# Last pair of the first deformable convolution: 24 halves and 13 gathered tiles in place of 16 and 17

## The chip, the cores and the metric

The kernel runs on one core of one Trainium2 chip. The metric is the time of one execution in microseconds (us), measured on the device. A core has five engines that work side by side, each through its own instructions in order, tied by semaphores: TensorE (PE in the rows, its weight loads PEld), VectorE (DVE), ScalarE (ACT), GpSimd (POOL) and SyncE (SP), which here only issues DMAs.

## The reference, cut to what matters

Two blocks work on 8 images of 32 channels and 80 x 80 pixels. The second has two deformable convolutions, here called C1 and C2; each samples, for each pixel and each of nine taps, the input at a place that a small convolution has computed, weighs it with a mask, and sums over taps and channels:

```python
def modulated_deform_conv(x, offset, mask, weight):
    ...
    py = ys - PAD + ki + off[:, :, 0]      # row of each tap's sample
    px = xs - PAD + kj + off[:, :, 1]      # column
    samp = bilinear_gather(x, py, px)      # four corners, weighted
    samp = samp * mask[:, None]
    return jnp.einsum('bckhw,ock->bohw', samp, weight.reshape(Co, Cx, KK))

om1 = conv2d(x, w_om1, b_om1)
out = modulated_deform_conv(x, offset1, mask1, w_dcn1)     # C1
out = jax.nn.gelu(batchnorm(out, ...))
out = modulated_deform_conv(out, offset2, mask2, w_dcn2)   # C2
x = x + jax.nn.gelu(batchnorm(out, ...) + identity)
```

## The kernel before

The images are worked on as four pairs (p = 0 to 3). In C1 a pair's pixels are sampled in one of two ways.

A **gathered tile** has 16 x 16 pixels of both images. GpSimd fetches the four corners of each sample from a table in memory with 36 indirect DMAs (L900), nine for each of four units, into one set of buffers G; a unit's buffer is free again when VectorE has summed the unit. VectorE computes the places (`locate`, `index`, `weigh`) two tiles ahead, multiplies the corners by their weights (L2139, `scale`) and adds them in pairs (L2153, `part`); TensorE turns and adds the parts (L1157, `turn_unit`), ScalarE copies the sample (L1542), TensorE projects it (L1244, `project_tile`).

A **half** has two rows of 64 pixels of both images and no gather. Offsets reach a few rows and columns only, so TensorE multiplies, for each tap, column weights TX1 (loaded by DMA and shaped by ScalarE, L1489 and L1491) with the columns of the table XT1 (`taps_half`, L1216; BTP are its two PSUM banks, one for each side). VectorE multiplies the 15 rows that come out by row weights TY1 (`weight_half`, L2250) into a product buffer for each side, and TensorE sums over the rows in transposing matmuls (`reduce_half`, L1229, 15 of them for each side and group of three taps). ScalarE copies the sample (L1712), TensorE projects it (`project_half`, L1253). Offsets, mask and row weights of two halves are made at a time (`prepare_half_strips`, L1898 to L1916; convolution L1091 and L1097, turning L1040).

Which pixels are halves is in `C1_ROWS`: for each pair a range of rows, columns 0 to 63. Rows 32 to 63 of the last pair make 16 halves; the other 17 tiles are gathered.

The order is written by hand: `schedule` calls, for every engine, the same list of steps, and `mix` reads a string. "g" is a gathered tile alone (`consume`), "f" a gathered tile with a half beside it, their instructions interleaved (`consume_both`), "d" and "x" belong to the first block's dense convolution, which is over before the last pair. The last pair's strings before are "gf", "ff", "ff", then three times "fff", then "ff"; behind each but the last stand three of the nine steps (`build_step`, L968) that build a table for C2. Behind the stage come `unlend`, `calibrate` and `columns`, and then C2's rounds, each with a gathered tile and a strip.

Of the kernel before, what the change touches and what calls it, by code (L numbers as in the profile page):

```python
# [9 lines left out]
PAIRS = 4  # L10
P = IMG * C
R2 = 2 * C
# [37 lines left out]
C1_ROWS = {0: (32, 48), 1: (32, 48), 2: (32, 48), 3: (32, 64)}  # L50
# [22 lines left out]
def build_program(nc, x, w_off, b_off, w_dcn, par, ident_d, base_y_d, base_x_d, bbase_d, out):  # L73
# [10 lines left out]
    with ctx:  # L84
# [60 lines left out]
        def lender(p):  # L145
            return 1 if p == 0 else 0
# [6 lines left out]
        TX1F = {p: [lent(lender(p), lent_at(p) + 128 * k0, 128 * (k1 - k0)) for k0, k1 in TX_TAPS] for p in C1_ROWS}  # L153
        TX1 = {p: lent(lender(p), lent_at(p), 128 * TAPS).rearrange("p (k b n) -> p k b n", k=TAPS, b=2) for p in C1_ROWS}
        TY1 = {p: lent(lender(p), lent_at(p) + 1152, IDXS * WY1).rearrange("p (n w) -> p n w", w=WY1) for p in C1_ROWS}
# [60 lines left out]
        TAP = BTP + [OUT[1]]  # L216

# [139 lines left out]
        def column_groups(p):  # L357
            first, end = C1_ROWS[p]
            r0, r1 = first - 1 - BELOW1, end + 1 + WY1 - 1 - BELOW1
            return r0, [(r, min(8, r1 - r)) for r in range(r0, r1, 8)]  # L360
# [64 lines left out]
        def mix(on, c, kinds, gseg, at, dseg, at_d, cseg, at_c, then=""):  # L425
            before = ()
            for i, kind in enumerate(kinds):
                seg = dseg if kind == "d" else gseg
                done = sum(k != "d" for k in kinds[:i])
                done_d = sum(k in "dx" for k in kinds[:i])  # L430
                t = done_d + at_d if kind == "d" else done + at
                halves = at_c + kinds[:i + 1].count("f")
                ahead = (cseg, halves) if (kinds + then)[i + 1:i + 2] == "f" else None
                closes = i + 1 == len(kinds)
                prep = after_next(seg, t, c.n)
# [66 lines left out]
        def schedule(eng, on):  # L502
# [14 lines left out]
            for p in C1_ROWS:  # L517
# [155 lines left out]
        def _(sp):  # L673
# [93 lines left out]
            class on:  # L767
# [40 lines left out]
                def consume_both(step, half):  # L808
                    if half.prep:
                        on.prepare(*half.prep)  # L810
# [126 lines left out]
        def _(pe):  # L937
            class on:
# [265 lines left out]
                def taps_half(half, k):  # L1204
# [5 lines left out]
                    if h or k:  # L1210
                        pe.wait_ge(weighted1, 18 * h + 2 * k)
                    row = strip_row(seg, t // 2) + t % 2 * 2 + k // 3 - 1 - BELOW1 - r0
                    for side in range(2):
                        ps_ = slice(XW * side, XW * side + XW)
                        for im in range(2):
                            last = nc.tensor.matmul(BTP[side][64 * im:64 * im + 64, 0:TAPW1], TX1[p][ps_, k, im, :],  # L1216
# [31 lines left out]
                def project_half(half):  # L1248
                    pe.wait_ge(main.samp_ready, half.v + 8)
# [8 lines left out]
                def consume_both(step, half):  # L1258
# [35 lines left out]
                    on.project_half(half)  # L1294

# [141 lines left out]
        def _(act):  # L1437
            class on:
# [262 lines left out]

                def consume_both(step, half):
# [4 lines left out]
                    def half_sample(gr):  # L1707
                        act.wait_ge(prod_used, step.wg + 2 * (gr + 1) + GROUPS)
                        if gr == 0:
                            act.wait_ge(main.projected, step.v + 2)  # L1710
                        from_ = RED[1][0:TPG * C, 0:256].rearrange("p (h n) -> p h n", h=2)
                        last = nc.scalar.activation(SAMP1[half.seg.p][:, gr], from_, ACT.Copy)  # L1712
                        if gr < GROUPS - 1:
                            last.then_inc(group_sampled, 1)
                        else:
                            last.then_inc(main.samp_ready, 2)

# [3 lines left out]
                    half_sample(0)  # L1721
# [3 lines left out]
                    half_sample(1)  # L1725
# [6 lines left out]
                    half_sample(2)  # L1732
# [20 lines left out]
        def _(dve):  # L1753
# [15 lines left out]
            class on:  # L1769
# [104 lines left out]
                def columns1(p, built, halves):  # L1874
# [5 lines left out]
                    r0, groups = column_groups(p)  # L1880
                    for j, (row, count) in list(enumerate(groups))[1::2]:
# [4 lines left out]
                def prepare_half_strips(seg, t, q, n, cs):  # L1886
# [5 lines left out]
                    ty, lent_ = TY1[seg.p], LENT[seg.p]  # L1892
# [14 lines left out]
                    if cs:  # L1907
                        dve.wait_ge(weighted1, 36 * cs)
# [334 lines left out]
                def weight_half(half, k):  # L2243
                    gr, j, p = k // TPG, k % TPG, half.seg.p
                    for side in range(2):
                        at = 2 * gr + side
                        if j == 0:
# [4 lines left out]
                            in0=BTP[side][:, 0:TAPW1].rearrange("p (w c) -> p w c", w=WY1),  # L2252
                            in1=TY1[p][:, (half.t % 2 * 2 + side) * TAPS + k, :].unsqueeze(2).to_broadcast([128, WY1, C]),
                            op=ALU.mult).then_inc(weighted1, 1)

# [186 lines left out]
```

## Time and profile before

| | us |
|---|---|
| median of 3 runs | 6645.84 |
| lowest and highest | 6641.96, 6651.39 |
| the profiled execution | 6641.73 |
| its span | 6639.8 |
| busy: TensorE | 5752.4 (87%) |
| busy: GpSimd | 4601.9 (69%) |
| busy: VectorE | 4548.5 (69%) |
| busy: ScalarE | 2140.5 (32%) |

A busy share is an average over the whole span. What an edit in one stage is worth has to be read in that stage: which engine is never idle, and which wait ends last. The last pair of C1 begins with its first gather at 3448.6 us of the span and ends with its last half's projection at about 4240.8.

### The profile page before, as it was taken

To read this page: it belongs to the slowest core of one execution; us is meant where nothing else is said; L and a number is where in the kernel's file an instruction comes from. 1 tells how busy PE (TensorE), PEld (TensorE's weight loads), DVE (VectorE), ACT (ScalarE), POOL (GpSimd) and SP (SyncE) were. 2 spreads that over 40 slices of the span, in tenths; PEclk is the share of its full clock that TensorE was granted. 3 is DMA by queue.
4 is the path that set the end of the run, shared out by engine and by line. 5 is a ranking of instruction groups with operands and counts; after the bars stand their busy time and mean duration, and the time that the engine had idled before them with its cause. 6 is when DMAs were issued, how large, how long until landed. Compare 5 with 4: busy or idle time off the path is not lost. (4 is left out here: it accounts for less than half of the span.)

```text
span 6639.8 us, 129061 instructions
## 1 busy us (share of the span) xinstructions
PE 5752.4 (87%) x50305; PEld 4624.7 (70%) x50305; DVE 4548.5 (69%) x8684; ACT 2140.5 (32%) x3416; POOL 4601.9 (69%) x4765
## 2 busy tenths in 40 slices
PE   6997888987888988888977777799989989998996
PEld 6886776766777757777754555577767767776775
DVE  6886776866777857777854555577666766776775
ACT  1222222222222222222222222254434444443442
POOL 0005777777777777777777777777777777777776
PEclk9997999998999989999978888899989989998998
DMA  5333343435343433443332222333333333333333
GB/s 149 100 100 108 106 113 110 116 88 143 103 113 107 116 88 105 111 110 102 106 84 78 74 71 74 93 88 88 84 90 94 91 80 103 91 88 86 89 85 76
DMA packets 511330, 647.82 MB, mean 98 GB/s; under 512 B 118856, under 2 KB 414120, under 8 KB 502824
## 3 DMA queue, kind: packets, MB, share of 16 engines
q0 software_dynamic: 152064, 311.73, 18.6%
q1 hardware_dynamic: 358696, 328.04, 17.5%
q8 instruction: 412, 6.75, 0.4%
q14 instruction: 158, 1.29, 0.1%
HBM read 593.26 MB, written 46.15 MB: 96 GB/s over the span
## 5 line engine op out<-in xcount | busy, mean ns | idle before, releaser
L900 POOL DMA_INDIRECT G<-table,IDX x4752 | 4587.8, 965 | 1992.9 <-issue 1930.8
L2340 DVE TENSOR_TENSOR ARENA<-ARENA,OUT 128x864 f32<-128x864 f32 x936 | 937.9, 1048 | 130.6 <-PE RED L1142 97.8
L2139 DVE TENSOR_TENSOR G<-G,WPS 128x1152 f32<-128x1152 f32 x528 | 711.5, 1348 | 432.9 <-DMA G<-table,IDX 431.7
L1547 ACT ACTIVATE SAMP<-RED 96x384 f32<-96x384 f32 x688 | 335.4, 487 | 1907.2 <-PE RED L1365 815.8
L1142 PE MATMUL RED<-IDENT,ARENA 128*96 128x128 f32 x7344 | 880.6, 280 | 76.2 <-DVE ARENA L2340 76.2
L1142 PEld LDWEIGHTS RED<-IDENT,ARENA 128*96 128x96 f32 x7344 | 820.6, 129 | 121.1 <-issue 117.4
L1346 PE MATMUL BTP<-PAD,ARENA 80*128 x2304 | 744.9, 446 | 56.1 <-DVE ARENA L2132 29.5
L1091 PE MATMUL OFF<-PAD,ARENA 128*54 128x128 f32 (+1 forms) x10944 | 740.9, 293 | 19.5 <-ACT PAD L1447 6.8
L1091 PEld LDWEIGHTS OFF<-PAD,ARENA 128*54 128x54 f32 (+1 forms) x10944 | 659.9, 133 | 128.5 <-issue 98.9
L1216 PE MATMUL BTP<-X 64*64 64x480 f32 x2880 | 396.4, 621 | 199.5 <-DVE ARENA L2250 139.6
L1542 ACT ACTIVATE SAMP<-RED 96x384 f32<-96x384 f32 x448 | 218.3, 487 | 1068.6 <-PE RED L1157 547.9
L1346 PEld LDWEIGHTS BTP<-PAD,ARENA 80*128 80x128 f32 x2304 | 398.0, 193 | 185.7 <-issue 95.1
L1355 PE MATMUL RED<-IDENT,ARENA 128*96 128x128 f32 x3840 | 497.3, 277 | 0.0
L1355 PEld LDWEIGHTS RED<-IDENT,ARENA 128*96 128x96 f32 x3840 | 423.5, 127 | 83.1 <-DVE PAD L2132 22.4
L1172 PE MATMUL RED<-IDENT,ARENA 128*96 128x128 f32 x3888 | 458.0, 276 | 0.0
L1172 PEld LDWEIGHTS RED<-IDENT,ARENA 128*96 128x96 f32 x3888 | 424.8, 127 | 22.5 <-issue 22.0
L2250 DVE TENSOR_TENSOR ARENA<-BTP,X 128x480 f32<-128x480 f32 x504 | 317.8, 651 | 166.6 <-PE BTP L1216 115.7
L1346 PE MATMUL OUT<-PAD,ARENA 80*128 x1152 | 413.7, 441 | 0.0
L1229 PEld LDWEIGHTS RED<-IDENT,ARENA 128*96 128x96 f32 x2520 | 281.2, 130 | 120.5 <-issue 119.1
L1229 PE MATMUL RED<-IDENT,ARENA 128*96 128x128 f32 x2520 | 320.1, 282 | 47.3 <-DVE ARENA L2250 45.5
L2340 DVE TENSOR_TENSOR ARENA<-ARENA,WPS 128x864 f32<-128x864 f32 x312 | 314.0, 1047 | 56.2 <-PE RED L1142 56.2
L1521 ACT ACTIVATE OFFS<-OFF,BOFF 54x128 f32<-54x128 f32 (+1 forms) x512 | 185.3, 362 | 486.2 <-PE OFF L1091 402.6
(221 smaller groups left out, 7392.1 us busy)
## 6 DMA issues: line engine op xcount, KB each, us to landing
ARENA<-wtab SPq DMA_DIRECT2D x416, 400.0 KB
G<-table,IDX POOLq DMA_INDIRECT x4752
ARENA<-xo SPq DMA_DIRECT2D x96, 720.0 KB
table<-TB SPq DMA_DIRECT2D x64, 384.0 KB, 2.7
X<-xo SPq DMA_DIRECT2D x80, 160.0 KB
X<-xo SPq DMA_DIRECT2D x80, 128.0 KB
X<-x SPq DMA_DIRECT2D x3, 3200.0 KB, 19.0
out<-X SPq DMA_DIRECT2D x20, 320.0 KB
```

The costliest lines, as they stand in the source:

```text
L900: pool.indirect_dma_start(G[:, b, k, :], None, tables[seg.table], bass.IndirectOffsetOnAxis(ap=IDX[:, q, b * TAPS + k:b * TAPS + k + 1], a ...
L1091: last = nc.tensor.matmul(out_, WOFF[s][:, k, cols], in_, start=(k == 0), stop=(k == TAPS - 1 and not strip))
L1142: last = nc.tensor.matmul(RED[b % 2][0:TPG * C, gr * 128:(gr + 1) * 128], PROD[gr][:, sft, :], IDENT[:, :], start=(sft == 0), stop=(sft == ...
L1172: last = nc.tensor.matmul(RED[1][0:TPG * C, gr * 128:(gr + 1) * 128], PROD[gr][:, sft, :], IDENT[:, :], start=(sft == 0), stop=(sft == 8), ...
L1216: last = nc.tensor.matmul(BTP[side][64 * im:64 * im + 64, 0:TAPW1], TX1[p][ps_, k, im, :], XT1[p][ps_, im, row:row + WY1, :].rearrange("p ...
L1229: last = nc.tensor.matmul(out_, PRODS1[half.seg.p][side][:, w, :], IDENT[:, :], start=(w == 0), stop=(w == WY1 - 1), is_transpose=True)
L1346: nc.tensor.matmul(TAP[c % TAPB][:, 0:TAPW], TXB[tt][:, im, k, :], XT[:, bass.ds(bases[k] + (im * H + row) * C, TAPW)], start=True, stop=T ...
L1355: last = nc.tensor.matmul(RED[1][0:TPG * C, gr * 128:(gr + 1) * 128], PRODS[gr][:, w, :], IDENT[:, :], start=(w == 0), stop=(w == WY - 1), ...
L1547: nc.scalar.activation(SAMP[:, x], RED[x][0:TPG * C, 0:GROUPS * 128].rearrange("p (g n) -> p g n", g=GROUPS), ACT.Copy).then_inc(z.samp_re ...
L2139: nc.vector.tensor_tensor(out=slots, in0=slots, in1=WEIGHTS[q][:, b * TAPS:(b + 1) * TAPS, :].rearrange("p k s -> p (k s)").unsqueeze(2).t ...
L2250: nc.vector.tensor_tensor(out=PRODS1[p][side][:, :, j * C:(j + 1) * C], in0=BTP[side][:, 0:TAPW1].rearrange("p (w c) -> p w c", w=WY1), in ...
L2340: nc.vector.tensor_tensor(out=PROD[gr].rearrange("p (dy dx) (j c) -> p j dy dx c", dy=3, j=TPG), in0=win.rearrange("p j dy (dx c) -> p j d ...
```

## The change

In the last pair the rows of the halves go from 32 to 80 in place of 64: 24 halves, and 13 gathered tiles. The order becomes "gfh", five times "fhfh", then "fh", with three table builds behind each but the last. "h" is new: a half alone (`consume_half`). Its taps alternate between two pairs of PSUM banks (`TAPS_ALONE`: BTP, and RED[0] with OUT[1]), so a tap waits for the products of the one before the last. All even halves now stand beside a tile and all odd ones alone, so the offsets and row weights of the next two halves, made behind every odd half, are made in a lone half: between the sixth and the seventh tap on VectorE. The row weights have two buffers in this pair, TX1 and TY1 lie elsewhere, and eight rows of XT1 past the image's end are set to zero.

```diff
-C1_ROWS = {0: (32, 48), 1: (32, 48), 2: (32, 48), 3: (32, 64)}
+C1_ROWS = {0: (32, 48), 1: (32, 48), 2: (32, 48), 3: (32, 80)}
...
+        TX1_AT = {p: 5000 if p == PAIRS - 1 else lent_at(p) for p in C1_ROWS}
+        TY1_AT = {p: lent_at(p) if p == PAIRS - 1 else lent_at(p) + 1152 for p in C1_ROWS}
+        TY1[PAIRS - 1].append(arena(6236, IDXS * WY1).rearrange("p (n w) -> p n w", w=WY1))
...
+        TAPS_ALONE = BTP, [RED[0], OUT[1]]
...
-                    for k, kinds in enumerate(("gf", "ff", "ff")):
-                        mix(on, c, kinds, g, 2 * k, None, 0, s, max(0, 2 * k - 1), "f")
-                        builds_of(on, c, range(3 * k, 3 * k + 3), KB["t", PAIRS], GSEG[PAIRS], False)
-                    on.finished(ENDS[1])
-                    for k in range(3):
-                        mix(on, c, "fff", g, 6 + 3 * k, None, 0, s, 5 + 3 * k, "f")
-                        builds_of(on, c, range(3 * k, 3 * k + 3), KB["t", PAIRS + 1], GSEG[PAIRS + 1], False)
-                    mix(on, c, "ff", g, 15, None, 0, s, 14)
+                    tiles = halves = 0
+                    for k, kinds in enumerate(("gfh", "fhfh", "fhfh", "fhfh", "fhfh", "fhfh", "fh")):
+                        if k == 3:
+                            on.finished(ENDS[1])
+                        mix(on, c, kinds, g, tiles, None, 0, s, halves, "f" if k < 6 else "")
+                        tiles, halves = tiles + sum(kind != "h" for kind in kinds), halves + sum(kind != "g" for kind in kinds)
+                        if k < 6:
+                            builds_of(on, c, range(3 * (k % 3), 3 * (k % 3) + 3), KB["t", PAIRS + k // 3], GSEG[PAIRS + k // 3], False)
...
+                    def alone(k):
+                        if k == 1:
+                            pe.wait_ge(main.samp_ready, half.v + 2)
+                        on.taps_half(half, k, TAPS_ALONE[k % 2], 2 if k else 1)
+                    alone(0)
+                    alone(1)
+                    if half.prep:
+                        on.convolve(*half.prep)
+                    alone(2)
+                    alone(3)
+                    if half.prep:
+                        on.turn_offsets(*half.prep)
+                    on.reduce_half(half, 0, 0)
+                    alone(4)
+                    on.reduce_half(half, 1, 0)
+                    alone(5)
+                    on.reduce_half(half, 0, 1)
+                    alone(6)
+                    on.reduce_half(half, 1, 1)
+                    alone(7)
+                    alone(8)
+                    pe.wait_ge(main.out_read, half.u + 2)
+                    on.reduce_half(half, 0, 2)
+                    on.reduce_half(half, 1, 2)
+                    on.project_half(half, 4)
...
-                    if cs:
-                        dve.wait_ge(weighted1, 36 * cs)
+                    if cs >= bufs:
+                        dve.wait_ge(weighted1, 36 * (cs + 1 - bufs))
...
+                def consume_half(half):
+                    for k in range(TAPS):
+                        on.weight_half(half, k, TAPS_ALONE[k % 2])
+                        if k == 2:
+                            for tile_ in half.before:
+                                on.finish(*tile_)
+                        if k == 5 and half.prep:
+                            on.prepare(*half.prep)
```

How the instructions stand. On TensorE, before, the end of the stage's last round that prepares two halves (L1229 reductions and L1253 projection of the half, L1157 and L1244 the tile's, L1091 and L1097 the convolution of the next two halves' offsets, L1040 their turning):

```order
L1091 MATMUL OFF<-PAD,ARENA 54x128 x18
L1097 MATMUL OFF<-X 54x128 x2
L1244 MATMUL OUT<-SAMP,WDCN 32x128 x3
L1229 MATMUL RED<-IDENT,ARENA 96x128 x15
L1157 MATMUL RED<-IDENT,ARENA 96x128 x6
L1229 MATMUL RED<-IDENT,ARENA 96x128 x15
L1244 MATMUL OUT<-SAMP,WDCN 32x128 x3
L1040 MATMUL OFF<-IDENT,OFFS 64x2x27 x4
L1253 MATMUL OUT<-ARENA,WDCN 32x128 x6
```

The convolution and its turning stand at the round's end, with the tile's work between. Now, on TensorE, the first part of the last lone half that prepares others (L1234 taps, L1109 and L1115 that convolution, L1058 turning, L1247 reductions):

```order
L1234 MATMUL BTP<-X 64x480 x4
L1234 MATMUL RED<-X 64x480 x2
L1234 MATMUL OUT<-X 64x480 x2
L1109 MATMUL OFF<-PAD,ARENA 54x128 x18
L1115 MATMUL OFF<-X 54x128 x2
L1234 MATMUL BTP<-X 64x480 x4
L1234 MATMUL RED<-X 64x480 x2
L1234 MATMUL OUT<-X 64x480 x2
L1058 MATMUL OFF<-IDENT,OFFS 64x2x27 x4
L1247 MATMUL RED<-IDENT,ARENA 96x128 x15
L1234 MATMUL BTP<-X 64x480 x4
L1247 MATMUL RED<-IDENT,ARENA 96x128 x15
```

Taps stand next to each other, on two pairs of banks, and only the half's own work lies between the reductions. On VectorE, in the same lone half, the row weights (L1967 to L1985, nine instructions, of which the first and last are shown) have moved from the round's end to between two taps' products (L2319):

```order
L2319 TENSOR_TENSOR ARENA<-OUT,X 128x15x32
L1967 SCALAR_TENSOR_TENSOR X<-OFF,X 128x2x9
...
L1985 SCALAR_TENSOR_TENSOR ARENA<-ARENA,MASK 128x540
L2319 TENSOR_TENSOR ARENA<-BTP,X 128x15x32 x2
L2319 TENSOR_TENSOR ARENA<-RED,X 128x15x32
L2319 TENSOR_TENSOR ARENA<-OUT,X 128x15x32
L2319 TENSOR_TENSOR ARENA<-BTP,X 128x15x32 x2
```

Three taps' products stand behind them.

## Rows read from the trace of the kernel before

**Rows 1.** The page: span, busy time by engine, and the gathers' group.

```profile
span 6639.8 us, 129061 instructions
PE 5752.4 (87%) x50305; PEld 4624.7 (70%) x50305; DVE 4548.5 (69%) x8684; ACT 2140.5 (32%) x3416; POOL 4601.9 (69%) x4765
L900 POOL DMA_INDIRECT G<-table,IDX x4752 | 4587.8, 965 | 1992.9 <-issue 1930.8
```

**Rows 2.** Windows, gathers alone: stretch, length, busy (count), clock, DMA, GB/s.

```profile
3448.60:4229.90 781.30, 594.87 (x612) 0.86 0.28 74
```

**Rows 3.** Windows, all engines: two rounds, three builds, the stage's two parts.

```profile
core 0: us, PE busy (x) PEld busy (x) DVE busy (x) ACT busy (x) POOL busy (x), PEclk, DMA share, GB/s
675.21:707.30 32.09, 28.94 (x262) 19.12 (x261) 23.30 (x42) 7.32 (x14) 24.17 (x27) 1.00 0.30 83
3501.56:3551.09 49.53, 33.48 (x262) 21.64 (x260) 22.02 (x40) 9.87 (x17) 37.65 (x40) 0.88 0.24 64
3640.69:3648.40 7.71, 5.33 (x37) 5.04 (x37) 1.67 (x3) 4.18 (x8) 5.88 (x7) 0.68 0.46 143
3883.05:3917.94 34.89, 31.72 (x263) 20.98 (x265) 21.66 (x39) 7.89 (x14) 26.53 (x28) 0.91 0.33 90
3551.09:4240.78 689.69, 538.22 (x4437) 367.51 (x4437) 358.67 (x666) 171.97 (x308) 525.16 (x541) 0.88 0.28 75
```

**Rows 4.** Timeline, a clean round: start, us, engine, line, what, [idle before <-releaser].

```profile
684.34 1.04 PE L1216 MATMUL BTP<-X 64*64 64x480 f32 x8
685.31 1.84 PE L1229 MATMUL RED<-IDENT,ARENA 128*96 128x128 f32 x15
687.08 0.84 PE L1244 MATMUL OUT<-SAMP,WDCN 96*32 96x128 f32 x6
...
704.08 1.80 PE L1229 MATMUL RED<-IDENT,ARENA 128*96 128x128 f32 x15
...
705.97 0.38 ACT L1712 ACTIVATE ARENA<-RED 96x256 f32<-96x256 f32 x1 [1.21 <-PE RED L1229]
...
706.40 0.90 PE L1253 MATMUL OUT<-ARENA,WDCN 96*32 96x128 f32 x12
```

**Rows 5.** Timeline, third pair's end: two halves' offsets and row weights.

```profile
3323.10 2.20 PE L1091 MATMUL OFF<-PAD,ARENA 128*54 128x128 f32 x36
...
3325.59 0.84 PE L1244 MATMUL OUT<-SAMP,WDCN 96*32 96x128 f32 x6
...
3338.76 0.68 PE L1040 MATMUL OFF<-IDENT,OFFS 118*64 118x54 f32 x8
...
3339.38 1.49 PE L1253 MATMUL OUT<-ARENA,WDCN 96*32 96x128 f32 x12
...
3339.73 0.18 DVE L1898 SCALAR_TENSOR_TENSOR X<-OFF,X 128x18 f32<-128x18 f32 x1 [13.19 <-ACT MASK L1534]
...
3342.45 0.72 DVE L1916 SCALAR_TENSOR_TENSOR X<-X,MASK 128x540 f32<-128x540 f32 x1
```

**Rows 6.** Timeline, a clean round: tap, its two products, the next tap.

```profile
697.50 1.03 PE L1216 MATMUL BTP<-X 64*64 64x480 f32 x8 [0.75 <-DVE ARENA L2250]
...
698.57 0.66 DVE L2250 TENSOR_TENSOR X<-BTP,X 128x480 f32<-128x480 f32 x1 [0.46 <-PE BTP L1216]
699.15 0.65 DVE L2250 TENSOR_TENSOR ARENA<-BTP,X 128x480 f32<-128x480 f32 x1
...
699.85 1.04 PE L1216 MATMUL BTP<-X 64*64 64x480 f32 x8 [0.52 <-DVE ARENA L2250]
```

**Rows 7.** Timeline: the stage's last projection, and GpSimd's wait in C2's first round.

```profile
4239.89 0.90 PE L1253 MATMUL OUT<-ARENA,WDCN 96*32 96x128 f32 x12
...
4286.51 0.94 POOL L900 DMA_INDIRECT G<-table,IDX  x1 [11.37 <-DVE SUM L2160]
```

**Rows 8.** Dense stage's transposing matmuls (windows); a reduction at the lower clock (timeline).

```profile
332.00:498.00 166.00, 125.10 (x1084) 116.64 (x1083) 1.00 0.36 100
...
4233.26 3.41 PE L1229 MATMUL RED<-IDENT,ARENA 128*96 128x128 f32 x15 [7.13 <-DVE ARENA L2250]
```

More of the change, by code:

```diff
@@ L358, in column_groups @@
             first, end = C1_ROWS[p]
-            r0, r1 = first - 1 - BELOW1, end + 1 + WY1 - 1 - BELOW1
+            r0, r1 = first - 1 - BELOW1, min(H + 1, end + 1 + WY1 - 1 - BELOW1)
             return r0, [(r, min(8, r1 - r)) for r in range(r0, r1, 8)]
@@ L428, in mix @@
                 seg = dseg if kind == "d" else gseg
-                done = sum(k != "d" for k in kinds[:i])
+                done = sum(k not in "dh" for k in kinds[:i])
                 done_d = sum(k in "dx" for k in kinds[:i])
                 t = done_d + at_d if kind == "d" else done + at
-                halves = at_c + kinds[:i + 1].count("f")
-                ahead = (cseg, halves) if (kinds + then)[i + 1:i + 2] == "f" else None
+                halves = at_c + sum(k in "fh" for k in kinds[:i + 1])
+                ahead = (cseg, halves) if (kinds + then)[i + 1:i + 2] in ("f", "h") else None
                 closes = i + 1 == len(kinds)
+                if kind == "h":
+                    k = halves - 1
+                    prep = None
+                    if k % 2 and k + 1 < len(cseg.tiles):
+                        prep = (cseg, k // 2 + 1, 0, c.n, cseg.first // 2 + k // 2 + 1)
+                    half = Step(cseg, k, 0, c.u, c.v, c.u % 2, cseg.first + k, c.n, prep, before, closes, ahead, c.wg, False, c.built)
+                    on.consume_half(half)
+                    before = ((cseg, k, c.u, c.u % 2),)
+                    c.n += prep is not None
+                    c.half, c.u, c.v, c.wg, c.drain = c.half + 1, c.u + 1, c.v + 2, c.wg + 6, True
+                    continue
                 prep = after_next(seg, t, c.n)
@@ L808, in consume_both @@
                 def consume_both(step, half):
+                    on.consume_half(half)
+                def consume_half(half):
                     if half.prep:
@@ L1202, in consume_pair, with taps_half @@
                     on.project_pair(step, dense, UNITS - 1)
-                def taps_half(half, k):
+                def taps_half(half, k, banks=BTP, behind=1):
                     seg, t, p, h = half.seg, half.t, half.seg.p, half.i
@@ L1215, in taps_half @@
                         for im in range(2):
-                            last = nc.tensor.matmul(BTP[side][64 * im:64 * im + 64, 0:TAPW1], TX1[p][ps_, k, im, :],
+                            last = nc.tensor.matmul(banks[side][64 * im:64 * im + 64, 0:TAPW1], TX1[p][ps_, k, im, :],
                                                     XT1[p][ps_, im, row:row + WY1, :].rearrange("p w c -> p (w c)"),
@@ L1294, in consume_both, with consume_half @@
                     on.project_half(half)
+                def consume_half(half):
+                    for e in tb_evac:
+                        pe.wait_ge(e, half.built)
+                    for side, e in enumerate(xt1_evac):
+                        pe.wait_ge(e, column_evacs(half.seg.p, side))
+                    def alone(k):
[23 more added lines that the diff above has]
+                    on.project_half(half, 4)
                 def dense_done(u):
@@ L1700, in consume_pair, with sample_half, consume_half @@
                             on.tents1(*step.ahead, im)
+                def sample_half(half, gr):
+                    act.wait_ge(prod_used, half.wg + 2 * (gr + 1) + GROUPS)
+                    if gr == 0:
+                        act.wait_ge(main.projected, half.v + 2)
+                    from_ = RED[1][0:TPG * C, 0:256].rearrange("p (h n) -> p h n", h=2)
+                    last = nc.scalar.activation(SAMP1[half.seg.p][:, gr], from_, ACT.Copy)
+                    if gr < GROUPS - 1:
+                        last.then_inc(group_sampled, 1)
+                    else:
+                        last.then_inc(main.samp_ready, 2)
+                def consume_half(half):
+                    if half.prep:
+                        on.offsets(*half.prep)
+                    on.sample_half(half, 0)
+                    if half.prep:
+                        on.mask(*half.prep)
+                    on.sample_half(half, 1)
+                    if half.ahead:
+                        on.tents1(*half.ahead, 0)
+                    on.sample_half(half, 2)
+                    on.finish(half, 4)
+                    if half.ahead:
+                        on.tents1(*half.ahead, 1)
                 def consume_both(step, half):
@@ L1720, in consume_both @@
                     tile_sample(0)
-                    half_sample(0)
+                    on.sample_half(half, 0)
                     tile_sample(1)
@@ L1724, in consume_both @@
                         on.mask(*step.prep)
-                    half_sample(1)
+                    on.sample_half(half, 1)
                     tile_sample(2)
@@ L1731, in consume_both @@
                     tile_sample(3)
-                    half_sample(2)
+                    on.sample_half(half, 2)
                     if half.prep:
@@ L1880, in columns1 @@
                     r0, groups = column_groups(p)
+                    within = sum(count for _, count in groups)
+                    if within < lent_at(p) // R2:
+                        nc.vector.memset(XT1[p][:, :, within:, :], 0.0)
                     for j, (row, count) in list(enumerate(groups))[1::2]:
@@ L2241, in consume, with weight_half @@
                         on.finish(seg, step.t, u, po)
-                def weight_half(half, k):
+                def weight_half(half, k, banks=BTP):
                     gr, j, p = k // TPG, k % TPG, half.seg.p
```

32 lines of the change are left out of this document (13 added, 19 removed).

## The prediction

> **What bounds the kernel now.** I read the page first: TensorE is busy 87% of a span of 6639.8 us and GpSimd 69% [rows 1]. The 69% is misleading. Nearly all of it is one line, the indirect gathers of L900: 4752 of them, 965 ns each, and 1930.8 of the 1992.9 us of idle time before them is "issue", time in which GpSimd waited for nobody [rows 1]. So GpSimd is saturated wherever it gathers. In the stage that the change touches, the last pair of the first convolution, it issued 612 gathers (17 tiles of 36) in 781.3 us [rows 2]. That is 1.277 us for each and 46.0 us for a tile, and the stage moves at this pace: TensorE's granted clock is only 0.88 there and it is busy 538.2 of 689.7 us [rows 3].
>
> So the question is what sets the stage's length once gathers are taken away. For that I need TensorE's own time for a round, with no gather in the way. A round is one gathered tile with one half beside it (`consume_both`; "both" from here on). The clean one, in the first pair at full clock (1.00, which is 2.4 GHz), lasts 32.1 us, of which TensorE is busy 28.9 [rows 3]. TensorE takes its work strictly in program order, so a lone half cannot slide under a round; it comes before it or after it.
>
> **Part 1, what is removed: four gathered tiles.** That takes 4 x 36 = 144 gathers from GpSimd, 4 x 46.0 = 184 us of its time. This is a gain only as long as GpSimd sets the pace. Per round the new stage needs 46.0 us of GpSimd, and of TensorE one both and one lone half. I show below that these take 32 + 26 = 58 us. The gathers then hide under TensorE and the 184 us are not received.
>
> **Part 2, what is added: 12 lone halves, while 16 boths become 12.** No lone half exists in the trace, so I build it from the pieces of a round at full clock. From one start to the next, the matmuls of a tap take 685.31 - 684.34 = 0.97 us and a reduction of 15 matmuls 687.08 - 685.31 = 1.77 us [rows 4]. Nine taps are 8.7, six reductions 10.6, the half's projection is 0.9 [rows 4]. Since the "both" rounds now always carry an even half, the offsets of the next two halves are always made in a lone half: convolution 3325.59 - 3323.10 = 2.5 us, turning 3339.38 - 3338.76 = 0.6 [rows 5]. Sum without any wait: 23.3 us (20.2 for the last half, which prepares nothing).
>
> The new second bank pair removes most waits between taps, but four stand in the order that the change writes:
> - The fourth tap's products go into the buffer that the first group's reductions read (one product buffer for a side, two tap banks). They wait for the reduction of side 1, and the sixth tap, which reuses the fourth's banks, waits for them. Another engine sees a reduction after 705.97 - 704.08 = 1.89 us [rows 4], and a tap follows the weighing by 699.85 - 699.15 = 0.70 [rows 6]: 2.59 in place of 1.77, so 0.8.
> - The second group's reduction stands right behind its last tap. VectorE starts 698.57 - 697.50 = 1.07 us after a tap's start and TensorE goes on 0.70 later [rows 6]: 1.77 in place of 0.97, so 0.8.
> - The third group has the same, 0.8. VectorE comes to it late, because it makes the row weights between the sixth and the seventh tap, 3339.73 to 3342.45 + 0.72, which is 3.4 us [rows 5]; I count 0.1 for that, since two taps and two reductions of TensorE stand beside it.
> - The last sample is copied by ScalarE before the projection: 706.40 - 704.08 = 2.32 in place of 1.77, so 0.5 [rows 4].
>
> These make 3.0, and a lone half 26.2 us. The ends: 23.3 if every wait is hidden, and 30.4 if the second bank pair helped nothing where two taps stand together (first and second, third and fourth, eighth and ninth), where the single-bank cycle is 699.85 - 697.50 = 2.35 in place of 0.97 [rows 6], 3 x 1.4 = 4.2 more. I take 26.2, because each of the four waits is written in the order.
>
> **Part 3, the second buffer of row weights and the moved tensors.** The row weights were made at the end of a round, behind everything else on VectorE; now they stand within a lone half, for the pair after next, and wait there for ScalarE's mask. Behind that wait on VectorE stand the last three taps' products, and TensorE's ninth tap waits for them. That is the 0.1 above. The seventh group of columns and the memset of eight rows of the column table come once, while the first gathered tile of the stage is still being fetched. I cost them at nothing. If that cover were gone they would cost about 2 us. The loads of the next half's column weights keep their place behind the fifth and ninth taps, as in a round.
>
> **The sum.** The stretch up to the end of the first both (3501.56 to 3551.09) waits for its gather and stays [rows 3]. Behind it stand, in the new stage, 12 lone halves, 11 boths and 6 groups of three table builds, all in a row on TensorE:
> - lone halves: 12 x 26.2 - 3.1 (the last prepares nothing) = 311
> - boths: 11 x 32.1 = 353 [rows 3]
> - six of them follow builds and start at half clock: the row of such a round shows 34.9 at 0.91 in place of 32.1 [rows 3]. I take 2.5 each, 15
> - builds: 6 x 7.7 = 46 [rows 3]
>
> Together 725 us. The same stretch took 689.7 before [rows 3]. The stage gets **35 us longer**.
>
> What comes behind moves with it, one to one. From the last projection to the first sum of the second convolution lie 45.7 us of calibration and columns, and GpSimd, with a whole tile fetched, stood 11.37 us there waiting for that sum [rows 7]. It is ahead already before the change; being further ahead gives nothing, since there is one set of gather buffers. I see no second stage that changes.
>
> The profiled execution took 6641.7 us (span 6639.8). With 35 us more it is 6677. The median shown is 4 us above the profiled one, which gives about **6680 us** against the 6645.8, or +0.5%.
>
> **Rivals.**
> A, not slower: the waits of a lone half all vanish, because VectorE runs ahead by the second bank pair. Place: the six reductions. Price: 2.9 us for each of 12 halves, 35 us, which is just the loss: 6645. The point from which it decides is a lone half of 23.3 us; any shorter one, or boths below their 32.1, makes the kernel faster. For it speaks that VectorE needs only 18 x 0.58 (698.57 to 699.15) + 3.4 = 14 us of the 26 [rows 5, 6]; against it, that the waits are of latency and order, not of VectorE's load.
>
> B, GpSimd keeps the pace: then 184 us go and the time is about 6462. It needs both and lone half within 46.0 us. Against it: the busy time of a clean both alone is 28.9 [rows 3], the lone half's pieces are 23.3, 52 in all.
>
> C, the clock: in a lone half 10.6 of 23 us are transposing reductions. If these ran at the lower level, 1.2 GHz, a reduction would take 3.41 us, as it does in the last round before the second convolution, in place of 1.80 [rows 4, 8]. 12 x 6 x 1.6 = 115 more give 6795. Against it: in the dense stage 1084 transposing matmuls fill 125.1 of 166 us at a granted clock of 1.00 [rows 8]. The Trainium skill, "TensorE: Matmul & The Clock Gate", Part 4 (PE-mode transpose), says that transposes do not count as activity in the same way and that the full clock does not engage for them; by that rule C would be the forecast, and 6795 the time. The trace disagrees with the rule, at the 1.00 just named, so I give C little.
>
> **How the numbers follow.** Forecast 0.74 (slower), A 0.14 (0.10 within the bound, 0.04 faster by a little), B 0.04 (faster), C 0.08 (slower). Faster or slower is counted from 0.2%, 13 us, about what a measurement of this kernel can tell from no change. So faster 0.08, same 0.10, slower 0.82. The forecast's own spread: lone halves 25 to 28 us (12 x -1.2 to +1.8: -14 to +22), the cold starts 0 to 3 us (-15 to +3), boths half a microsecond either way (6). That is about 6655 to 6705. Of the ends above, 30.4 us for a lone half would be 6730 and 23.3 would be A's 6645; the range takes in most of A and part of that upper end: 6650 to 6712.
>
> **What will show it.** GpSimd's line has 4608 gathers, and in the stage it stands idle about 12 us a tile, with VectorE's sums as the releaser. TensorE is busy about 90% of the stage at a clock near 0.95. From one both's start through a lone half to the next both is 58 us. If it is 46, B holds; if lone halves last about 23, A; if their taps or reductions take twice the time, C. The prediction is wrong as a whole if the second convolution's first sum does not move with the stage's end.

## The result, and the profile after

The changed kernel takes 6673.58 us (median of 5 runs, 6668.98 to 6682.49) against 6647.95 us (median of 5, 6641.96 to 6651.39) on the same chip: a ratio of **1.0043**, 95% interval 1.003 to 1.0057. The profiled execution took 6668.98 us. Slower by some 26 us, where 34 us slower had been forecast (6680 against 6645.8).

The page of the changed kernel, its rows that answer to [rows 1]:

```profile
span 6667.2 us, 131732 instructions
PE 5841.3 (88%) x51581; PEld 4676.2 (70%) x51581; DVE 4605.8 (69%) x8781; ACT 2187.2 (33%) x3475; POOL 4451.9 (67%) x4621
L918 POOL DMA_INDIRECT G<-table,IDX x4608 | 4437.8, 963 | 2168.9 <-issue 1878.2
```

GpSimd lost 144 gathers and 150 us of busy time, as the change says. TensorE gained 89 us of busy time, and the span grew by 27.4.

The windows view by stage (start:end, length, busy us with counts by engine, TensorE's granted clock, DMA share, GB/s). In this order: the first both, the stage from there to the last projection, one clean both, the lone half behind it, the group of three table builds behind that, the both behind the builds, and the tail up to the second convolution's first sum. Both and lone half run from the end of one half's projection to the end of the next.

```profile
core 0: us, PE busy (x) PEld busy (x) DVE busy (x) ACT busy (x) POOL busy (x), PEclk, DMA share, GB/s
3502.14:3552.25 50.11, 35.36 (x265) 23.43 (x266) 22.17 (x40) 9.87 (x17) 37.92 (x41) 0.80 0.25 64
3552.25:4271.77 719.52, 632.13 (x5681) 422.65 (x5681) 411.38 (x762) 219.32 (x367) 403.18 (x423) 0.96 0.25 68
3771.79:3803.82 32.03, 28.87 (x263) 19.06 (x267) 21.54 (x39) 10.19 (x18) 19.09 (x21) 1.00 0.23 59
3803.82:3829.75 25.93, 22.59 (x223) 14.71 (x223) 13.96 (x27) 8.60 (x15) 15.32 (x16) 1.00 0.26 67
3829.75:3837.03 7.28, 5.21 (x37) 4.87 (x37) 1.67 (x3) 3.77 (x7) 0.00 (x0) 0.72 0.27 100
3837.03:3871.91 34.88, 31.71 (x263) 20.98 (x266) 21.54 (x39) 7.89 (x14) 19.09 (x21) 0.91 0.24 66
4271.77:4316.19 44.42, 30.31 (x211) 23.86 (x211) 16.24 (x65) 14.99 (x16) 0.00 (x0) 0.62 0.34 110
```

The stage went from 689.69 us [rows 3] to 719.52, **29.8 us longer**, which accounts for the result (the span grew by 27.4). TensorE is busy 88% of it, where it was 78% of it before (538.22 of 689.69). GpSimd went the other way, from 525.16 busy to 403.18. The waits view of GpSimd, from 3480 to 4330 us (engine, what, line, releaser: us in total, times, longest):

```profile
POOL G L918 <- DVE SUM L2222: 189.9, 22, 23.0
POOL G L918 <- issue: 142.6, 468, 0.3
POOL G L918 <- DVE SUM L2229: 49.0, 1, 49.0
```

In the kernel before, the same view of its stage (3551 to 4240 us) has next to nothing of this; GpSimd goes on without waiting for anybody:

```profile
POOL G L900 <- issue: 164.2, 539, 0.3
POOL G L900 <- DVE SUM L2153: 0.3, 1, 0.3
```

The waits on VectorE's sums of gathered tiles (L2222) mean that GpSimd has its buffers full and stands until TensorE's round lets the next tile be consumed. The 49.0 us are the second convolution's first sum: GpSimd was further ahead there than before (11.37 us, [rows 7]) and got nothing for it.

The timeline of TensorE in the lone half above (start, us, engine, line, operation, count, [idle before it <- what released it]), the rows with a wait:

```profile
3815.57 0.62 PE L1234 MATMUL RED<-X 64*64 64x480 f32 x2 [0.84 <-DVE ARENA L2319]
...
3817.43 1.81 PE L1247 MATMUL RED<-IDENT,ARENA 128*96 128x128 f32 x15 [0.83 <-DVE ARENA L2319]
...
3824.92 3.45 PE L1247 MATMUL RED<-IDENT,ARENA 128*96 128x128 f32 x30 [1.15 <-DVE ARENA L2319]
...
3828.90 0.85 PE L1271 MATMUL OUT<-ARENA,WDCN 96*32 96x128 f32 x12 [0.53 <-ACT ARENA L1758]
```

They are the four waits of the prediction, at its four places: the sixth tap, the second group's first reduction, the third group's, the projection. Together 3.35 us, where 3.0 had been worked out.

### The profile page after: what moved, and what is told of

Same layout as the page of the kernel before. It is cut to its first block and busy times, and to the rows that moved or that the text cites. A ratio compares the mean times of both kernels' runs of the same rounds, so it can differ in the third digit from the quotient of the medians.

```text
span 6667.2 us, 131732 instructions
## 1 busy us (share of the span) xinstructions
PE 5841.3 (88%) x51581; PEld 4676.2 (70%) x51581; DVE 4605.8 (69%) x8781; ACT 2187.2 (33%) x3475; POOL 4451.9 (67%) x4621
## 5 line engine op out<-in xcount | busy, mean ns | idle before, releaser
L918 POOL DMA_INDIRECT G<-table,IDX x4608 | 4437.8, 963 | 2168.9 <-issue 1878.2
L1160 PE MATMUL RED<-IDENT,ARENA 128*96 128x128 f32 x7344 | 876.7, 279 | 76.8 <-DVE ARENA L2420 76.8
L2208 DVE TENSOR_TENSOR G<-G,WPS 128x1152 f32<-128x1152 f32 x512 | 690.1, 1348 | 342.9 <-DMA G<-table,IDX 341.5
L1160 PEld LDWEIGHTS RED<-IDENT,ARENA 128*96 128x96 f32 x7344 | 817.2, 129 | 121.1 <-issue 118.0
L1109 PE MATMUL OFF<-PAD,ARENA 128*54 128x128 f32 (+1 forms) x10944 | 729.8, 291 | 15.1 <-ACT PAD L1498 6.8
L1109 PEld LDWEIGHTS OFF<-PAD,ARENA 128*54 128x54 f32 (+1 forms) x10944 | 650.0, 131 | 119.3 <-issue 101.8
L1234 PE MATMUL BTP<-X 64*64 64x480 f32 x3072 | 413.4, 609 | 169.4 <-DVE ARENA L2319 109.7
L1406 PE MATMUL RED<-IDENT,ARENA 128*96 128x128 f32 x3840 | 497.4, 277 | 0.0
L1406 PEld LDWEIGHTS RED<-IDENT,ARENA 128*96 128x96 f32 x3840 | 423.5, 127 | 83.0 <-DVE PAD L2201 24.2
L1190 PE MATMUL RED<-IDENT,ARENA 128*96 128x128 f32 x3888 | 455.7, 275 | 0.0
L1247 PEld LDWEIGHTS RED<-IDENT,ARENA 128*96 128x96 f32 x3240 | 350.7, 127 | 135.7 <-issue 125.5
L1190 PEld LDWEIGHTS RED<-IDENT,ARENA 128*96 128x96 f32 x3888 | 422.8, 127 | 21.7 <-issue 21.4
L1247 PE MATMUL RED<-IDENT,ARENA 128*96 128x128 f32 x3240 | 396.4, 276 | 33.4 <-DVE ARENA L2319 30.9
L2319 DVE TENSOR_TENSOR ARENA<-BTP,X 128x480 f32<-128x480 f32 x384 | 244.2, 651 | 136.2 <-PE BTP L1234 92.5
```

The costliest lines, as they stand in the source:

```text
L918: pool.indirect_dma_start(G[:, b, k, :], None, tables[seg.table], bass.IndirectOffsetOnAxis(ap=IDX[:, q, b * TAPS + k:b * TAPS + k + 1], a ...
L1109: last = nc.tensor.matmul(out_, WOFF[s][:, k, cols], in_, start=(k == 0), stop=(k == TAPS - 1 and not strip))
L1160: last = nc.tensor.matmul(RED[b % 2][0:TPG * C, gr * 128:(gr + 1) * 128], PROD[gr][:, sft, :], IDENT[:, :], start=(sft == 0), stop=(sft == ...
L1190: last = nc.tensor.matmul(RED[1][0:TPG * C, gr * 128:(gr + 1) * 128], PROD[gr][:, sft, :], IDENT[:, :], start=(sft == 0), stop=(sft == 8), ...
L1234: last = nc.tensor.matmul(banks[side][64 * im:64 * im + 64, 0:TAPW1], TX1[p][ps_, k, im, :], XT1[p][ps_, im, row:row + WY1, :].rearrange(" ...
L1247: last = nc.tensor.matmul(out_, PRODS1[half.seg.p][side][:, w, :], IDENT[:, :], start=(w == 0), stop=(w == WY1 - 1), is_transpose=True)
```

## The experiments

The theory under test: before, the stage goes at GpSimd's pace; after, at TensorE's, whose own work with 12 lone halves of 26 us is longer than the stage was at GpSimd's pace. The main rival: one engine sets the pace in both kernels. All times of a stage below run from the end of the first both to the last projection (689.69 us before, 719.52 after). The kernel before took medians between 6644 and 6661 us on the chips used, so whole times are compared as ratios to it.

**The changed kernel once more.**

> The changed kernel once more, on the chip of the three runs beside it, so that they can be set against it directly. Expected: ratio to the kernel before 1.003 to 1.006; the stretch from the first both's end to the last projection 719.5 us within 2.

Ratio 1.0044 (1.0029 to 1.0058); the stage 719.68 us. As expected. The span was 6674.5, 7 us more than in the first profile, and all of that lies ahead of the stage (the first both ended at 3559.37, not 3552.25). So the stage repeats to 0.2 us while the whole execution moves by several.

**Fewer gathers, in the changed kernel.** (`GSEG[PAIRS - 1]` is the last pair's gathered tiles.)

```diff
-                    for k in range(TAPS):
+                    for k in range(5 if seg is GSEG[PAIRS - 1] else TAPS):
```

> The changed kernel, with 5 instead of 9 gathers for each unit of the last pair's 13 tiles: 208 of 4608 gathers left out, some 260 us of GpSimd's time, and the four taps not fetched are summed from what an earlier tile left in the buffer. Theory (TensorE is the pace of this stage now, GpSimd waits in it): the stage from the first both to the last projection stays 719 us within 5 us, the time stays 6674 us within 12, and GpSimd only waits longer. Rival (GpSimd still sets a good part of the stage, its waits being short ones that the sums cause): the stage falls by 100 us or more, to a time below 6570 us.

Windows, the first both and the stage:

```profile
3493.48:3531.46 37.98, 32.42 (x265) 20.98 (x266) 21.95 (x41) 10.33 (x18) 25.80 (x28) 0.87 0.25 63
3531.46:4250.75 719.29, 631.83 (x5682) 422.33 (x5681) 411.45 (x762) 219.14 (x367) 226.65 (x240) 0.96 0.18 51
```

176.5 us of GpSimd's work left the stage and the stage stayed at 719.29. So GpSimd has no part in its pace. The whole time did fall, though, to a ratio of 1.0011 (0.9999 to 1.0022), some 20 us, which I had not expected: the first both took 37.98 instead of 50.11 and began 9 us earlier. There the stage's first tiles are fetched while TensorE waits, so gathers still count at that one place.

**The same, in the kernel before.**

> The kernel before, with 5 instead of 9 gathers for each unit of the last pair's 17 tiles: 272 gathers left out, some 345 us of GpSimd's time, the four taps not fetched summed from what an earlier tile left. Theory (GpSimd was the pace of this stage before, and what the change takes from it can't be received beyond TensorE's own length): the stage of 689.7 us falls to TensorE's length and no further, 575 to 600 us (boths of 32.1 us, preparations, builds and restarts), so that the time is 6535 to 6560 us, and the gap of GpSimd's load that is left over shows as waiting on VectorE's sums. Rival (TensorE was already the pace before, at 40 us for a both): the stage stays at 690 us within 5 us and the time at 6648 us.

Ratio 0.9897 (0.9861 to 0.9933), the stage 636.48 us. Windows for the stage, then the waits of GpSimd, TensorE and ScalarE in it; last, SyncE's queue in the same stage of the kernel before:

```profile
3539.44:4175.92 636.48, 519.67 (x4438) 352.81 (x4437) 355.84 (x666) 171.88 (x308) 288.18 (x304) 0.89 0.21 56
...
POOL G L900 <- DVE SUM L2154: 251.2, 30, 24.7
...
PE OUT L1244 <- ACT SAMP L1542: 53.7, 7, 7.8
...
ACT X L1489 <- DMA X<-xo: 66.3, 7, 9.6
...
SPq L830 <- ACT OFFS L1521: 253.5, 7, 45.6
```

The direction holds: gathers taken from the kernel before shorten its stage by 53 us, and GpSimd then begins to wait (251.2 us). But I had expected 575 to 600 us and got 636. The rows name what I missed; no run takes it away alone. Seven times, in each both that prepares the next two halves, ScalarE waits up to 9.6 us for the load of the next half's column weights. Its last samples stand behind that wait, and TensorE's projection stands up to 7.8 us for them, 53.7 us in all; without these the stage would be at some 583 us, an estimate (636.5 - 53.7), within what I had expected. The load is late because SyncE issues it behind the transport of the new offsets (L830), which it reads, and those exist only near that both's end: seven waits of SyncE's queue, up to 45.6 us in the kernel before and up to 34.1 in this run. In the kernel before the same waits are there:

```profile
ACT X L1489 <- DMA X<-xo: 62.7, 7, 9.3
...
PE OUT L1244 <- ACT SAMP L1542: 30.3, 6, 7.5
```

They lay under GpSimd's 46 us a tile and cost nothing. In the changed kernel there is no such row: the preparing now stands early in lone halves. So the change also removed a stall of TensorE's that stood in the rows before without setting the time.

**One pair of tap banks in lone halves.** The second side's first reduction also goes ahead of the fifth tap, since the products need its place.

```diff
-        TAPS_ALONE = BTP, [RED[0], OUT[1]]
+        TAPS_ALONE = BTP, BTP
...
-                        on.taps_half(half, k, TAPS_ALONE[k % 2], 2 if k else 1)
+                        on.taps_half(half, k, TAPS_ALONE[k % 2], 1)
...
-                    alone(4)
                     on.reduce_half(half, 1, 0)
+                    alone(4)
```

> The changed kernel with the lone halves' taps in the two banks of the boths again (the second pair of banks undone, each tap waiting for the product of the tap before it, and the second side's first reduction ahead of the fifth tap, since the products need its place). Theory: with one pair of banks each tap waits for VectorE's product of the tap before, some 0.5 to 0.8 us at six of the nine taps, so that a lone half takes 29 to 31 us instead of 26, the stage grows by 40 to 60 us and the time comes to 6715 to 6735 us. Rival (the second pair of banks hides nothing, the lone half is the sum of TensorE's pieces either way): stage and time unchanged within 6 us.

Ratio 1.0185 (1.0141 to 1.0229), the stage 819.01 us: 99.5 us longer, twice what I expected. Windows for the stage, a lone half that kept the full clock and one that didn't; then TensorE's waits in the stage, and in a lone half (the same in these two):

```profile
3551.36:4370.37 819.01, 660.95 (x5681) 435.19 (x5681) 415.24 (x762) 219.12 (x367) 400.08 (x424) 0.94 0.22 60
3834.94:3867.40 32.46, 23.27 (x223) 14.58 (x223) 14.23 (x27) 8.59 (x15) 14.91 (x16) 1.00 0.21 54
4115.00:4151.88 36.88, 27.70 (x223) 17.43 (x223) 14.32 (x27) 8.59 (x15) 14.90 (x16) 0.86 0.18 47
...
PE BTP L1234 <- DVE ARENA L2319: 117.6, 117, 1.5
...
PE BTP L1234 <- DVE ARENA L2319: 7.0, 6, 1.5
PE RED L1247 <- DVE ARENA L2319: 1.7, 2, 0.8
PE OUT L1271 <- ACT ARENA L1758: 0.5, 1, 0.5
```

The 99.5 us are 74.6 us more of taps waiting for products (117.6 here, 43.0 in the changed kernel), 28.8 us more of busy time at a lower granted clock, and 3.7 us less of the reductions' waits. Each lone half now stands 9.2 us instead of 3.35, and in ten of the twelve the clock falls (0.85 to 0.95). One such row, the third group's 30 matmuls in the lone half behind the first both:

```profile
3578.99 4.98 PE L1247 MATMUL RED<-IDENT,ARENA 128*96 128x128 f32 x30 [0.84 <-DVE ARENA L2319]
```

against 3.45 us above. So the second pair of banks, with the order that it allows and the clock that it keeps, is worth 8.3 us in each lone half (99.5 / 12), and the change stands on it.

**Shorter reductions in lone halves.**

```diff
-                    for w in range(WY1):
+                    for w in range(rows_):
...
-                    on.reduce_half(half, 0, 0)
+                    on.reduce_half(half, 0, 0, 5)
```

> The changed kernel with the lone halves' reductions over 5 of their 15 rows (two thirds of these sums are left out of the result): 60 of 90 transposing matmuls less in each of 12 lone halves. Theory (the stage passes a lone half's length on in full, and the reductions are TensorE work at full clock of some 0.12 us a row and side and group, less what new waits on VectorE take back): a lone half falls from 26 us to 20 to 21.5 us, the stage by 55 to 70 us, the time to 6605 to 6620 us, that is below the kernel before. Rival 1 (VectorE's products are what a lone half lasts as long as, and the shorter sums turn into waits): a lone half stays at 25 us or more, and the time falls by no more than 12 us. Rival 2 (GpSimd takes over as the pace at 46 us a round): the stage falls by less than 30 us because GpSimd no longer waits.

Ratio 0.9958 (0.9947 to 0.9969), the stage 667.33 us: 52.2 us below the changed kernel's, a little short of the 55 to 70. Windows for the stage, a clean lone half and a both behind a slower one, TensorE's waits in the stage, and the ninth tap's row in that lone half:

```profile
3556.61:4223.94 667.33, 565.14 (x4961) 349.04 (x4961) 411.09 (x762) 219.35 (x367) 403.21 (x423) 0.94 0.27 73
3790.12:3811.07 20.95, 16.24 (x163) 8.15 (x163) 13.91 (x27) 8.60 (x15) 15.24 (x16) 1.00 0.33 83
3641.79:3675.45 33.66, 30.51 (x263) 19.95 (x266) 21.64 (x39) 9.79 (x17) 19.39 (x20) 0.95 0.22 56
...
PE BTP L1234 <- DVE ARENA L2319: 51.1, 56, 1.7
...
3806.55 1.03 PE L1234 MATMUL BTP<-X 64*64 64x480 f32 x8 [1.67 <-DVE ARENA L2319]
```

The lone half's length decides, and at 21 us the kernel is faster than before. 67.0 us of TensorE's work left and 52.2 arrived. The difference is a new wait: the ninth tap now stands 1.67 us, 11 times, because VectorE makes the row weights (3.4 us) and there is too little TensorE work beside them (18.2 us of taps' waits more, 3.4 of reductions' waits less). The work left is itself less than the clean lone half promises: in three of the twelve the granted clock fell behind these waits, they took 22.1 to 22.7 us in place of 21 and the boths behind them 33.1 to 33.7 in place of 32.0, some 8 us together. TensorE's work beside the row weights is the cover that the prediction named in its third part; it is there in the changed kernel and gone here.

**One buffer of row weights.**

```diff
-        TY1[PAIRS - 1].append(arena(6236, IDXS * WY1).rearrange("p (n w) -> p n w", w=WY1))
...
-                        if k == 5 and half.prep:
-                            on.prepare(*half.prep)
+                    if half.prep:
+                        on.prepare(*half.prep)
```

> The changed kernel with one buffer for the last pair's row weights, which are then made behind the ninth tap's products of the lone half instead of between the sixth and the seventh (the second part of the change undone). Theory: VectorE makes them in 3.4 us, and behind the last product it has 3.5 us of reductions, 0.5 of waiting and 0.85 of projection on TensorE before the next group's first tap, so that nothing waits for it: each lone half stays at 25.6 us, or gets 0.3 us shorter as the third group's reductions wait 0.8 instead of 1.15 us; stage unchanged within 5 us. Rival (the row weights stand in TensorE's way at the end of a lone half): 3 to 4 us for each of 11 lone halves, a stage longer by 30 to 45 us.

Ratio 1.0051 (1.0034 to 1.0068), the stage 719.91 us, a lone half 25.93 us: nothing changed. Made at the end of the lone half, the row weights are hidden under the last reductions just as well. So this part of the change is worth nothing by itself. The third group's wait stayed at 1.15 us here, so the part of it over 0.83 is not the row weights' doing. The rows of the changed kernel show what it is: the eighth and the ninth tap stand together on TensorE, 0.86 us from start to start (3821.92 and 3822.78), while VectorE takes 1.14 us for the eighth tap's products (3822.99 to 3824.13), so that it begins the ninth's 0.3 us late.

**The builds spread over the steps.** Each of 18 successive steps holds one table build, behind its last reduction; the groups between the rounds are gone.

```diff
+                    mix(on, c, "g" + "fh" * 12, g, 0, None, 0, s, 0, "", {k + 2: what for k, what in enumerate(steps)})
...
                     on.reduce_half(half, 1, 2)
+                    build_within(on, half)
                     on.project_half(half, 4)
```

> The changed kernel with the 18 table builds of the stage no longer in six groups of three between the rounds, but one in each of 18 successive steps (both or lone half), behind the last reduction and ahead of the last projections. Theory (TensorE is the pace, so what it waits for in the builds and the half clock behind them are lost in full): six groups of 7.3 us and six cold boths of 2.0 to 3.2 us more go, 44 + 15 us; 18 builds of 12 matmuls come back at some 0.9 to 1.2 us each, 16 to 22, and the projections' waits are filled. The stage falls from 719.5 to 675 to 690 us and the time by 30 to 45 us against the changed kernel, ratio to the kernel before 0.997 to 1.000. Rival (a build within a step makes ScalarE or VectorE late for the samples and products, 1 to 2 us in each step): no gain, the stage at 710 us or more.

> The same, and in the lone halves the first group's second reduction is put ahead of the fifth tap, and the second group's two reductions behind the seventh tap. Theory: the sixth tap no longer waits 0.84 us for the fourth tap's products, nor the second group's reduction 0.83 us for its last tap's, some 1.0 to 1.6 us of a lone half's 25.6: the stage 12 to 19 us below the one with the builds spread alone, ratio to the kernel before 0.995 to 0.998. Rival (the waits only move to the taps behind the reductions): within 5 us of the one with the builds spread alone.

And the same for the kernel before:

> The kernel before, with its 18 table builds of this stage spread in the same manner over 14 of its 16 boths (two in each of the first four, one in each of the next ten) instead of in six groups of three between them. Theory (GpSimd's gathers are the pace of this stage before, TensorE is the pace of it after): what gave 32 us in the changed kernel gives next to nothing here, since TensorE's time saved is not received; the stage stays at 680 to 692 us, the ratio to the kernel before 0.998 to 1.0005. Rival (the groups of builds stop the stage whatever sets its pace): 32 us or more here too, a stage of 658 us or less and a ratio of 0.995 or less.

Ratios: 0.9996 (0.9986 to 1.0005) with the builds spread, **0.9961** (0.9947 to 0.9975) with the lone half's order changed too, and 1.0 (0.9991 to 1.001) for the kernel before with its builds spread. Windows for the three stages, in that order; then GpSimd's waits for VectorE's sums in the last of them:

```profile
3557.51:4244.96 687.45, 616.73 (x5681) 413.84 (x5681) 411.46 (x762) 219.14 (x367) 405.06 (x423) 1.00 0.27 71
...
3557.49:4226.92 669.43, 614.67 (x5681) 414.92 (x5681) 410.63 (x762) 219.14 (x367) 401.19 (x424) 1.00 0.27 73
...
3553.18:4240.23 687.05, 535.44 (x4437) 367.75 (x4437) 359.19 (x666) 171.22 (x308) 522.49 (x541) 0.90 0.29 75
...
POOL G L907 <- DVE SUM L2162: 0.9, 3, 0.3
```

The same kind of edit takes 32.1 us from the changed kernel's stage and 2.6 us from the other one. That separates the theory from its rival: here a pause of TensorE is paid for where TensorE sets the pace, and next to nothing where GpSimd does. In the kernel before TensorE only waits elsewhere (its reductions 66.2 us for products in place of 38.4), and GpSimd, with 0.9 us of waiting in 687, goes on as it did.

Where the 32.1 come from: a group of builds and the cold both behind it (one that begins at the lower clock) took 7.28 + 34.88 = 42.16 us, all six 250.1, and six clean boths take 192.2, so 57.9 go (the stage's clock is 1.00 now). The 18 builds come back at 1.17 us in most of the nine lone halves and 1.75 in most of the nine boths, 25.8 in all instead of the 16 to 22 expected. In a lone half the build fills the 0.53 us for which the projection had to wait. The new order of a lone half,

```diff
                     on.reduce_half(half, 0, 0)
-                    alone(4)
                     on.reduce_half(half, 1, 0)
+                    alone(4)
                     alone(5)
-                    on.reduce_half(half, 0, 1)
                     alone(6)
+                    on.reduce_half(half, 0, 1)
                     on.reduce_half(half, 1, 1)
                     alone(7)
```

takes 18.0 us more, 1.5 for a lone half. TensorE's waits in a lone half of that kernel:

```profile
PE RED L1252 <- DVE ARENA L2328: 0.8, 1, 0.8
PE BTP L1239 <- DVE ARENA L2328: 0.6, 2, 0.4
```

1.4 us are left of 3.35; the projection's 0.53 is filled by the build. This version beats both kernels: its median is 6620.36 us, beside 6644.09 for the kernel before and 6673.37 for the changed one in the same comparison.

## Why the prediction was right

**What bounds the kernel.** Right. The two runs with fewer gathers and the two with spread builds show it from both sides: GpSimd before, TensorE after.

**Part 1, the four tiles.** Right: 144 gathers went and nothing of their 184 us was received. From one both's start to the end of the lone half behind it are 32.03 + 25.93 = 57.96 us (58 said), and GpSimd waits 12.9 us in a round without builds (12 said).

**Part 2, the lone half.** 25.93 us against 26.2. The four waits are 3.35 instead of 3.0, the pieces 22.6 instead of 23.3 (turning the offsets spaces 0.38 us, not 0.6, and two taps that stand together 0.86, not 0.97). The second bank pair, which no trace had shown, does what was assumed. Only the upper bound for it was too low: without it a lone half takes 32.5 to 36.9 us, not 30.4. At the full clock it is already 32.5, since six taps wait, 7.0 us in all, where the bound had counted four, 5.0; the rest is the clock, which fell and which the bound had left out.

**Part 3, row weights.** Nothing, as costed. The reason given for 0.1 us (VectorE late by the row weights) was wrong, as the run with one buffer shows: the third group waits 1.15 us either way, behind the eighth tap's products. The ninth tap, which was to wait for them, has no wait in the changed kernel. What comes once (the seventh group of columns, the memset) can't be told apart: the first both ended 1.2 us later than before, and two profiles of one kernel differ by 7 there. No run shows the 2 us that it was to cost without its cover.

**The sum.** Working from end to end: 12 lone halves 309.3 us (311 said), 11 boths with six groups of builds and six cold starts 410.2 (353 + 46 + 15 = 414). Together 719.5 against 725. The term that was most off is the builds, 43.6 us for 46: 7.3 us a group behind a lone half instead of 7.7. The cold starts were 14.3 us for 15. The loss is 29.8 instead of 35, and the profiled execution 6669.0 for 6677.

**The tail.** It moves with the stage's end: the last projection 31.0 us later, the second convolution's first sum 29.7 (4316.19 against 4286.51 in [rows 7]). The span grew by 27.4; the 2 us between are less than two profiles of one kernel differ ahead of the stage.

**The rivals.** A needed lone halves of 23.3 us. Measured, the break-even is 25.9 - 29.8 / 12 = 23.4 us, and the waits stayed; the run with shorter reductions went below it and was faster. B fell with GpSimd's waits. C, transposing reductions at the lower clock, fell too: a lone half's reductions, 90 of its 223 matmuls, take 1.81 us for 15 at a granted clock of 1.00, not 3.41 [rows 8]. The Trainium skill, "TensorE: Matmul & The Clock Gate", Part 4 (PE-mode transpose), says that the full clock doesn't engage for transposes; in this kernel they ran at it, between taps and other matmuls, and the measurement decides. Whether transposes alone would raise the clock no run shows.

**What could still have surprised.** The prediction built the new stage from a clean both, and never said why the boths of the stage before, 35 to 48 us long, would all become clean. They did, since GpSimd's pace is off them and the late load that stalls seven of them (the run of the kernel before with fewer gathers) is gone with the change. Had the preparing stayed in the boths, a stall of up to 7.8 us at each that prepares would by that run's rows have been on the path; no run of the changed kernel tests this. It isn't in the sum, which was right here partly by luck: the same omission put the expected stage of that run at 575 to 600 us, and it was 636.

## What to carry to other kernels

Find for each stage the engine that sets its pace, and build the length of the changed stage from that of the next engine, piece by piece, before counting what the first one saves: a saving is received only down to the second engine's length. When a change moves the pace to another engine, look again at every pause of that engine that used to be free; here the pauses for table builds, worth 3 us before, were worth 32 after, and taking them out with a better order of the lone halves turned a loss of 0.4% into a gain of 0.4%. And look for waits of the second engine that the first one hides: they come with its pace.

## What the runs showed of the hardware that was not expected

- In these runs the granted clock fell with waiting inside otherwise dense work. With 3.35 us of waits in 25.9, all lone halves kept a granted clock of 1.00. With 4.7 in 21 (the shorter reductions, the eleven that prepare others), eight did and three fell to 0.90 to 0.92. With 9.2 in 32 to 37 (the single pair of banks, again the eleven), nine fell (0.86 in the one shown) and two stayed at 1.00, with the same waits. There the lower clock added 28.8 us of busy time to 74.6 us of waits over the stage.
- A stretch of 687 us without the pauses for builds ran at 1.00 throughout, where six pauses of 7.3 us had brought it to 0.96.
